# One step of skew in the joined tail block, and two of eight picks weighted on VectorE

## The reference, cut to what matters

```python
# L2 ffn: 4 heads, 128 keys a side, the best 8 of 4096 experts per head and token
scores, pk = top_k(all_scores, 8); indices = take_along_axis(all_indices, pk)
w   = silu(einsum('btd,bthkd->bthk', hidden, down_embed[indices])) * softmax(scores)
out = einsum('bthk,bthkd->btd', w, up_embed[indices]) + (silu(h @ Wg.T) * (h @ Wu.T)) @ Wd.T
x = layernorm(x + out)
# L3 attn: state-space, per sequence
v_local = depthwise_conv3(silu(v)); scan h = a*h + b*v_t; y = c*h + d*v_t
out = layernorm((u * silu(y)) @ out_proj + residual) * ln_w + ln_b;  x = layernorm(x + out)
# L3 xattn: 8 heads of 64 over 120 context tokens
x = layernorm(x + softmax(q k^T / 8) v @ Wo + bo)
```

## Time and profile before

| | us |
|---|---|
| runs of the kernel (3) | 3331.88 median, 3330.68 to 3333.36 |
| profiled execution | 3331.43 |
| its span, first to last instruction | 3329.5 |
| mean granted TensorE clock | 0.856 |
| busy: PE, PEld | 2408.2 (72%), 1613.7 (48%) |
| busy: DVE, ACT, POOL | 1604.5 (48%), 1152.2 (35%), 785.7 (24%) |

### The profile page before, as it was taken

One profiled execution on the slowest core, in us unless ns is written; L12 is line 12 of the kernel. 1 busy time (PEld: TensorE's weight loads), 2 busy tenths in 40 slices (PEclk: granted clock), 3 DMA queues, 4 the chain that ended last, 5 costly groups with the idle time before them and its releaser, 6 DMA issues. The chain is left out here.

```text
span 3329.5 us, 38556 instructions
## 1 busy us (share of the span) xinstructions
PE 2408.2 (72%) x14138; PEld 1613.7 (48%) x14145; DVE 1604.5 (48%) x4208; ACT 1152.2 (35%) x2006; POOL 785.7 (24%) x756
## 2 busy tenths in 40 slices
PE   6777699797776654768777656676777767677686
PEld 3534488544434324624444345555555555555432
DVE  3644200357437582456647643545444545432187
ACT  0233122200422321320245522455445455545343
POOL 1000200130010064510000065543444444530000
PEclk9888599899988777977998877888888888887798
DMA  7200255262043335543001251111111111100000
GB/s 171 63 18 0 105 184 180 75 144 83 23 86 110 127 123 186 161 146 57 11 17 63 90 113 38 38 40 28 34 31 37 34 31 40 33 22 13 13 0 25
DMA packets 127119, 232.26 MB, mean 70 GB/s; under 512 B 38809, under 2 KB 76569, under 8 KB 122592
## 3 DMA queue, kind: packets, MB, share of 16 engines
q1 hardware_dynamic: 73840, 125.12, 13.4%
q0 software_dynamic: 51952, 100.65, 10.1%
q10 hardware_dynamic: 1152, 4.19, 0.3%
HBM read 245.59 MB, written 66.72 MB: 94 GB/s over the span
## 5 line engine op out<-in xcount | busy, mean ns | idle before, releaser
L2827 POOL DMA_INDIRECT L2f_G<-in_L2f_table,L2f_idx x512 | 524.6, 1025 | 566.0 <-PE psum L2880 409.9
L2880 PE MATMUL psum<-L2f_G,L2f_diag 128*128 128x256 f32 x1024 | 340.8, 505 | 279.1 <-ACT L2f_diag L3077 279.1
L2880 PEld LDWEIGHTS psum<-L2f_G,L2f_diag 128*128 128x128 f32 x1024 | 262.3, 263 | 356.5 <-ACT L2f_diag L3077 293.8
L3257 DVE CUSTOM_DVE_ANT_0 L2f_junk<-L2f_G,L2f_X 128x256 bf16<-128x256 f32 x512 | 182.7, 421 | 1.7 <-DMA L2f_G<-in_L2f_table,L2f_idx 1.7
L3077 ACT ACTIVATE L2f_diag<-const,L2f_actd 128x128 f32<-128x128 f32 x528 | 161.2, 388 | 33.4 <-DVE L2f_actd L3270 33.4
L3263 DVE TENSOR_TENSOR L2f_h<-L2f_h,psum 128x256 f32<-128x256 f32 x64 | 26.9, 421 | 289.7 <-ACT L2f_h L3065 289.2
L1032 PE MATMUL psum<-constb 128*128 128x256 bf16 x512 | 81.9, 285 | 85.9 <-ACT L1a_PT L1199 24.8
L2251 POOL DMA_INDIRECT picks_x<-L1f_rows,L1f_put x64 | 70.8, 1107 | 242.1 <-ACT L1f_rows L2341 223.2
L2861 PE MATMUL psum<-xT,L2f_mw 128*128 128x256 f32 x512 | 123.3, 384 | 3.9 <-ACT L2f_X L3048 3.9
L1199 ACT ACTIVATE L1a_PT<-psum 128x1536 f32<-128x1536 f32 x32 | 46.4, 1451 | 207.1 <-PE psum L1167 207.1
L1512 PE MATMUL psum<-L0f_xeT,L0f_we 128*128 128x256 f32 x480 | 107.9, 384 | 0.9 <-DVE L0f_xeT L1547 0.9
(11 more groups left out here) (677 smaller groups left out, 5185.3 us busy)
## 6 DMA issues: line engine op xcount, KB each, us to landing
L1f_we<-in_L1f_w SPq DMA_DIRECT2D x32, 384.0 KB, 8.6
picks_x<-zeros SPq DMA_DIRECT2D x16, 544.0 KB, 9.1
L1f_xe<-picks_x SPq DMA_DIRECT2D x32, 272.0 KB, 2.8
picks_y<-zeros SPq DMA_DIRECT2D x16, 512.0 KB, 6.3
L2f_G<-in_L2f_table,L2f_idx POOLq DMA_INDIRECT x512, 2.8
slots_x<-zeros POOLq DMA_DIRECT2D x8, 512.0 KB, 7.6
L1f_wb<-in_L2x_w SPq DMA_DIRECT2D x1, 4096.0 KB, 12.1
L1f_g<-picks_y ACTq DMA_DIRECT2D x8, 512.0 KB, 12.7
```

What stands on the lines that cost most here:

```text
L2827: nc.gpsimd.indirect_dma_start(out=G[:, n % ROWS, :], out_offset=None, in_=ins["L2f_table"], in_offset=bass.IndirectOffsetOnAxis(ap=IDX[:, ...
L2880: mm = mm_(ps[:, MIX, 0:D], diag[:, i % 2, k, :], row[:, D:2 * D], start=(h == 0 and k == 0), stop=(h == HEADS - 1 and k == TOPK - 1))
L3257: e = VE.tensor_tensor_reduce(out=junk[:, k, :], in0=row[:, 0:D], in1=X[:, t % 4, :], scale=1.0, scalar=0.0, op0=ALU.mult, op1=ALU.add, ac ...
```

## The change

Every engine's order in a round is rewritten so that dots, small Silu, weights and diagonals of step i + 1 are done in round i; those of step 0 come ahead of the loop. Picks are TensorE's first work in a round; similar and queries follow them at once, and still wait for `gated`. VectorE puts the next step's dots ahead of `gated`. ScalarE has `gate` of this step first in its round.

Of the eight rows of a step, the last two (`OWN` = 6 on) are no longer turned into diagonals: VectorE multiplies them by their weights and adds them up over the four heads in a tile `rest` (`scaled`), with a semaphore `pk_scaled` that GpSimd also waits for. `keep` moves to VectorE and adds `rest` to what TensorE summed. The ninth row stays on TensorE.

ScalarE asks for its tables by name: one table with Ln and Exp, one with Silu, each when the last one asked for was the other.

```diff
+    OWN = 6
+        rest = sb("rest", [P, D])
+        def turned(i):
+            own = rows(i)
+            return [(k, own[k]) for k in range(len(own)) if not OWN <= k < TOPK]
 # gpsimd, before a gather into a used buffer
                             pool.wait_ge(s["pk_used"].sem, s["pk_used"].at((n - ROWS) // TOPK + 1))
+                            pool.wait_ge(s["pk_scaled"].sem, s["pk_scaled"].at((n - ROWS) // TOPK + 1))
 # tensor: picks
-                    for k, row in enumerate(rows(i)):
+                    for k, row in turned(i):
 # tensor: round i
-                    cross(i, 0)
-                    if h == 0 and 0 < t <= NT:
-                        turn_back(t - 1)
                     if i < STEPS:
+                        picks(i)
                         if h == 1 and t + 2 < NT:
                             pe.wait_ge(s["pk_hid"].sem, s["pk_hid"].at(i + 1))
...
+                    cross(i, 0)
                     ssm(i)
-                    if i < STEPS:
-                        picks(i)
-                    cross(i, 1)
+                    if h == 0 and 0 < t <= NT:
+                        turn_back(t - 1)
                     if i < STEPS:
                         pe.wait_ge(s["pk_hid"].sem, s["pk_hid"].at(i + 1))
                         down(i)
...
+                    cross(i, 1)
 # scalar
+                table = [""]
+                def tables(own):
+                    if own != table[0]:
+                        nc.scalar.preload_act_table_set(own)
+                        table[0] = own
+                LOGS, SILU = "natural_log_exp_and_others", "silu_and_others"
                 def inverse_root(bank, root, square, done):
+                    tables(LOGS)
                     link(nc.scalar.activation(root, ps[:, bank, 0:CW], ACT.Ln, bias=c.eps))
 # (in the same way before every Silu, Exp and Ln of the block)
 # scalar: round i
-                    if h == 0 and 0 < t <= NT:
-                        keep(t - 1)
                     if i < STEPS:
-                        weigh(i)
-                        diagonal(i)
-                    cross(i, 0)
+                        gate(i)
+                    if i + 1 < STEPS:
+                        weigh(i + 1)
+                        diagonal(i + 1)
                     if i < STEPS:
                         if h == 1 and t + 2 < NT:
                             evac_similar(t + 2)
...
+                    cross(i, 0)
                     ssm(i)
-                    cross(i, 1)
                     if i < STEPS and h == 3 and t + 2 < NT:
                         exps(t + 2)
-                    if i + 1 < STEPS:
-                        gate(i + 1)
+                    cross(i, 1)
 # vector
+                def scaled(i):
+                    t, h = divmod(i, HEADS)
+                    dve.wait_ge(s["pk_mix"].sem, s["pk_mix"].at(i + 1))
+                    if i:
+                        dve.wait_ge(s["pk_scaled"].sem, s["pk_scaled"].at(i))
+                    if h == 0 and t:
+                        dve.wait_ge(s["pk_ycopy"].sem, s["pk_ycopy"].at(t))
+                    for k in range(OWN, TOPK):
+                        row, by = rows(i)[k][:, D:2 * D], act_d[:, i % 2, k:k + 1]
+                        if h == 0 and k == OWN:
+                            e = VE.tensor_scalar(rest[:, :], row, by, None, ALU.mult)
+                        else:
+                            e = VE.scalar_tensor_tensor(rest[:, :], row, by, rest[:, :], ALU.mult, ALU.add)
+                        if k + 1 < TOPK:
+                            link(e)
+                    e.then_inc(s["pk_scaled"].sem, 1)
+                def keep(t):
+                    dve.wait_ge(s["pk_used"].sem, s["pk_used"].at((t + 1) * HEADS))
...
+                    VE.tensor_tensor(mix[:, :], ps[:, MIX, 0:D], rest[:, :], ALU.add).then_inc(s["pk_ycopy"].sem, 1)
 # vector: round i
-                    if i < STEPS:
-                        gated(i)
-                    ssm_gate(i)
-                    if i < STEPS:
-                        dot(i)
-                    late = cross_at(i, 0)[1] == 10
-                    if not late:
-                        cross(i, 0)
-                    if i < STEPS:
-                        weighted(i)
-                    if late:
-                        cross(i, 0)
+                    ssm_gate(i)
+                    if i + 1 < STEPS:
+                        dot(i + 1)
+                    if i < STEPS:
+                        gated(i)
+                    if i + 1 < STEPS:
+                        weighted(i + 1)
+                    if i < STEPS and h == HEADS - 1:
+                        keep(t)
+                    if i + 1 < STEPS:
+                        scaled(i + 1)
                     if h == 0 and 0 < t <= NT:
                         add_mix(t - 1)
...
+                    cross(i, 0)
                     ssm(i)
```

More of the change, by code:

```diff
@@ L2878, in picks @@
                         pe.wait_ge(s["pk_ycopy"].sem, s["pk_ycopy"].at(t))
-                    for k, row in enumerate(rows(i)):
+                    for k, row in turned(i):
                         mm = mm_(ps[:, MIX, 0:D], diag[:, i % 2, k, :], row[:, D:2 * D],
-                                 start=(h == 0 and k == 0), stop=(h == HEADS - 1 and k == TOPK - 1))
+                                 start=(h == 0 and k == 0), stop=(h == HEADS - 1 and k == OWN - 1))
                     mm.then_inc(s["pk_used"].sem, 1)
@@ L3064, in gate @@
                         act.wait_ge(s["pk_part"].sem, s["pk_part"].at(i - 1))
+                    tables(SILU)
                     nc.scalar.activation(h_[:, i % 2, :], ps[:, UP, 0:CW], ACT.Silu).then_inc(s["pk_silu"].sem, 1)
@@ L3075, in diagonal @@
                         act.wait_ge(s["pk_used"].sem, s["pk_used"].at(i - 1))
-                    for k in range(len(rows(i))):
+                    for k, row in turned(i):
                         e = nc.scalar.activation(diag[:, i % 2, k, :], c.ident, ACT.Copy, scale=act_d[:, i % 2, k:k + 1])
                     e.then_inc(s["pk_diag"].sem, 1)
-                def keep(t):
-                    act.wait_ge(s["pk_used"].sem, s["pk_used"].at((t + 1) * HEADS))
-                    if t:
-                        act.wait_ge(s["pk_yturn"].sem, s["pk_yturn"].at(t))
-                    nc.scalar.copy(mix[:, :], ps[:, MIX, 0:D]).then_inc(s["pk_ycopy"].sem, 1)
                 def inverse_root(bank, root, square, done):
+                    tables(LOGS)
                     link(nc.scalar.activation(root, ps[:, bank, 0:CW], ACT.Ln, bias=c.eps))
@@ L3163, in _ @@
                 evac_queries(2)
-                gate(0)
+                weigh(0)
+                diagonal(0)
                 act.wait_ge(s["padded"].sem, s["padded"].at(3))
```

10 lines of the change are left out of this document (8 added, 2 removed).

## The result

The changed kernel takes 3206.8 us (median of 4 runs, 3203.6 to 3213.1) beside 3332.6 (3330.7 to 3340.5) for the kernel before: ratio 0.962, 95% interval 0.960 to 0.964. That is 126 us less; 210 were forecast. Its profiled execution took 3205.7 us, span 3203.9, granted clock 0.854. A kernel's time here is the median of its fast runs; one of e2's four ran at a lower granted clock (0.784 for 0.85) and took 3350.8 us, and is left out.

A forecast was written before the change was run, and what follows sets the result against it. The prediction took a ring of engines, each waiting for the next and none full, to bound the kernel. Gains of 28 + 39.5 + 119 + 23 = 209.5 us off 3331.4 gave 3122 us, range 3060 to 3220.

The forecast's parts named there:

- Rival B: Named table loads come on top of the program's own, in steps and tail: 3204 us; chance 0.07.
- The ring is cut: Next step's dots to diagonals run during this step, so picks find diagonals ready; 125.0 us per eight steps against 142.4.
- the walk: Following four engine queues in their new order, pricing each step and wait: 120.7 us per eight steps at full clock.
- Rival C: The walk is too strict; eight steps take 105 us, halfway to the gather rate: 3005 us; chance 0.11.
- Steps 8 to 16, 39.5: Steps with state-space work but no cross-attention: 88 us against 127.5, so 39.5 us gained.
- Up to step 8, 28: First steps, paced by the gathers: gate product of step 8 at 2018 us against 2046, so 28 us gained.
- Steps 16 to 63, 119: Middle steps with cross-attention: 718 us against 836.8, so 119 us gained.
- Part 2: Two of eight picks on VectorE, not diagonals and matmuls: costs 2 us per eight steps (bounds 0.5 and 9).
- Part 3: ScalarE's tables asked for by name: some 11 loads leave the chain behind step 63, 14 us gained; 14 per eight steps.
- Step 63 and after, 23: Block's end: 14 us gained from fewer table loads, 9 from step 63 having no dots, best pairs or late diagonals.
- Rival A: Head-of-line waits eat the skew where cross-attention runs; steps 16 to 63 stay at 17.8 us each: 3241 us; chance 0.14.
- Rival D: TensorE falls to the lower clock level and becomes the bound: 3380 us, slower; chance 0.06.

The follow-up runs named there:

- e2: The changed kernel with tables no longer asked for by name, so the program puts in its own loads: 3265.7 us, ratio 0.978 to the kernel before.
- e7: The changed kernel with 12 extra TensorE matmuls after the picks of each tile's second and third step: 3241.3 us, ratio 0.970 to the kernel before.
- f1: The changed kernel with 20 row buffers in place of 28: 3190.4 us, ratio 0.956 to the kernel before.
- e1: The changed kernel with all eight picks as diagonals and TensorE matmuls again, nothing scaled on VectorE: 3209.4 us, ratio 0.962 to the kernel before.
- e3: The changed kernel with each named table load ahead of its activation's wait on ScalarE: 3191.2 us, ratio 0.956 to the kernel before.
- e6: The changed kernel with cross 0, ssm and turn_back ahead of similar and queries on TensorE: 3189.8 us, ratio 0.954 to the kernel before.

## Why the prediction was right and where it failed

It was right in sign and in the mechanism of the gain; the gain came out at three fifths of the forecast. 3206.8 lies outside the forecast's own bounds (3075 to 3175) and inside the stated range only because this reached toward the rivals. Rival B's 3204 is nearly the measured time, by chance: its mechanism is absent, as shown below. By its steps:

- **The ring is cut.** Right: picks hardly wait for diagonals (15.4 us in all), most of TensorE's waiting ends on the gate product, GpSimd still waits. The wait of 6 us for `add_dense` was in no step of the walk, but step 0 took the 13.3 us that the walk gave it (13.5). Rival C (bound by the gathers at 13 us a step) is out for the middle steps.
- **Steps 8 to 16, 39.5.** Wrong, 9.4. From first dot to first dot, as the walk counts, the rounds 8 to 14 took 16.2, 7.9, 23.7, 14.4, 15.4, 9.0 and 18.5 us, where it gave 10.6, 6.0, 14.5, 8.3, 13.7, 7.9 and 15.3: 21 us too much in rounds 8, 10 and 11 alone. These are the spells at 2032 to 2042 and 2080 to 2088 and, between them, the round in which `up` ends 5.6 us before ScalarE goes on. The step that failed is "hops between engines cost 0.04": in the trace of the changed kernel ScalarE goes on 2.2 to 13.2 us after the end of the `up` that it waits for in steps 1, 3, 6 and 10. In the trace that the prediction was read from ScalarE goes on 0.03 us after `up`, as it assumed; what makes the difference stays open, and how much of the 30 us is late semaphores and how much are chains that the walk missed was not taken apart. The sum of the shortest times that these steps had in any of the eleven traces of the new order is 89.9, but such a sum is too low by its making: for steps 0 to 8 it gives 69.9, less than the 82.5 that the rate of the gathers allows (product 0 at 1935.5, product 8 at 2018 at the earliest).
- **Up to step 8, 28.** Wrong in the same way, 12.4. The 80th gather was issued at 2022.0, not at 2012.5, since GpSimd too stood waiting in the spells (4.8 us behind the first 36 gathers), and the product came 11.6 us behind it, not 5.5.
- **Steps 16 to 63, 119.** 86.4. Per eight steps 132.5 for 125.0. By i mod 8 from 0 the walk gave 13.5, 11.1, 20.3, 15.9, 15.6, 7.5, 22.4 and 14.4; measured from dot to dot are 13.3, 17.0, 21.9, 15.4, 14.9, 9.6, 26.7 and 13.7, with the longest at 2 and 6 as forecast. Too short were 1 (by 5.9), 2 (1.6), 5 (2.1) and 6 (4.3). Of these the forecast had set aside 2.15 each for the clock in 1 and 5, which is all of 5. In 1 the clock costs 4.6 (e7), not 2.15, since V, mean and more ran slowly too. In 6, 3.5 go away with the late semaphore (f1; 3.0 from product to product), again the hop. The rest, some 3.7 us in 1, 2 and 6 against 2.1 that the other steps were shorter, no run took apart.
- **Part 2.** Costed at 2 us per eight against what ScalarE and TensorE save: no effect (e1). Right.
- **Part 3.** 14 us behind step 63: 14.8 (e2). The time is right, the count is not: 25 loads stood there and 5 are left, so 20 went and not 11, and 14.8 of their 25.7 us lay on the path. Per eight steps 14 loads, as counted, for 21 before. (By load and drain together, as the Trainium skill has them in "ScalarE: Activation LUTs", What ACT_TABLE_LOAD costs, the prediction's 11 loads would make an estimate of 29; the runs don't show the drain: Exp starts 0.01 us behind a load.) There is no load between Ln and Exp, so rival B is out. "A named load comes behind its wait" was right too: 108.7 us of idleness ahead of the loads; but charging each to the path was harsher than e3's gain bears out.
- **Step 63 and after, 23.** 19.4, near enough.
- **Rival A** (head-of-line waits eat the skew) had a mechanism that costs: e6 gives back 0.8%, about as much as f1. Its price, all of the middle gain, was wrong. **Rival D** (TensorE at the lower level as the bound) is out: 0.84 over the stretch, and no engine full.

## What to carry to other kernels

Where a ring of engines is cut, an asynchronous stream that the ring had paced (here GpSimd's gathers) comes in longer runs; look at the lengths of these runs before and after, and try fewer buffers as well as more (20 for 28 gained 0.7% here). After such a change read each engine's wait against the end of what it waits for, not only the name of the releaser: a gap of microseconds there is a cost that no instruction's duration shows. Where such gaps show, trace the kernel before again too: here its first trace had none and its second had some. And place a named table load ahead of the wait (0.6% here), and a matmul that must wait behind those that need not (0.8%).

## What was unexpected of the hardware

In the later traces TensorE's semaphores arrived 2 to 6 us late while 9 to 12 gathers in a row were being issued, and 0.02 us after the end when the last gather was 5 us old or it was the first of a run. In the first trace of the kernel before they arrived within 0.2 us even inside a run of 44. In the early steps of the changed kernel even dots without a wait were 0.7 to 2.8 us apart, the first time while the DMA engines were busy for 0.6 to 0.96 of the time, as they were at the same place in that first trace, which has no such spell. What inside the chip holds them back was not settled. Nor was how far the recording of a run takes part: the traces with late semaphores hold 21,002 to 22,351 semaphore updates, that of the kernel before in its second trace too (21,531), where its first one has 27,899; and "remote" in these views often only means that the update's record is missing. The kernel before took 3331 to 3333 us when its first trace was made and 3336 to 3342 (medians) beside the experiments, so the executions themselves may differ, and not only their records.
